# One unrolled phase for the convolution-style attention layer and the token attention with its dispatch

## The reference

```python
x = _L0_conv_ref(x, ...)                    # window attention, 8 heads
x = _L1_conv_ref(x, ...)                    # this change
t = _to_tokens(x)
t = t + _L2_attn_ref(_ln_t(t))              # this change
t = t + _L2_ffn_ref(_ln_t(t), ...)          # routing: this change; experts: later phase
t = t + _L3_attn_ref(_ln_t(t), ...)
t = t + _L3_ffn_ref(_ln_t(t), ...)
...
def _L1_conv_ref(...):
    h_ = group_norm(x, gn_scale, gn_bias)   # 32 groups of 4 channels
    q, k, v = conv1x1(h_, wq, bq), conv1x1(h_, wk, bk), conv1x1(h_, wv, bv)
    attn = softmax(einsum('bci,bcj->bij', q, k) * c ** -0.5)
    return x + conv1x1(einsum('bij,bcj->bci', attn, v), wp, bp)
def _L2_attn_ref(x):
    return softmax(x @ x.T) @ x             # per image, on normalized tokens
def _L2_ffn_ref(...):                       # top 2 of 8 experts, gates by softmax over the two
    topk_vals, topk_idx = top_k(x @ Wg + bg, 2)
```

## Time and profile before

| | |
|---|---|
| median of 3 runs | 2289.88 us (2289.37 to 2290.26) |
| span of the profiled execution, first to last instruction | 2284.1 us |
| PE, DVE, ACT, POOL busy, share of the span | 78%, 71%, 61%, 62% |
| conv phase, from its first ACT instruction to that of d2 | 391.87 to 561.50 us |
| d2 phase, to the first ACT instruction of moe2 | 561.50 to 877.17 us |

### The profile page before, as it was taken

One profiled execution on the slowest core, in us unless ns is written; L12 is line 12 of the kernel. 1 busy time (PEld: TensorE's weight loads), 2 busy tenths in 40 slices (PEclk: granted clock), 3 DMA queues, 4 the chain that ended last, 5 costly groups with the idle time before them and its releaser, 6 DMA issues. The chain is left out here.

```text
span 2284.1 us, 52612 instructions
## 1 busy us (share of the span) xinstructions
PE 1787.9 (78%) x16257; PEld 1236.1 (54%) x16257; DVE 1618.3 (71%) x4634; ACT 1404.3 (61%) x3208; POOL 1414.1 (62%) x1485
## 2 busy tenths in 40 slices
PE   7999997998777744777764777777786299999974
PEld 3555554776566643555543344444444177777763
DVE  5888887787677643666654588888786378888864
ACT  5777775564666523555540788888885267777750
POOL 3655554010177773777776378888888557767765
PEclk9999998999989857999985898998897599999995
DMA  6000000000221134666647012111110367777748
GB/s 116 17 0 0 0 0 2 1 0 18 74 83 55 55 89 124 185 180 179 174 122 249 9 60 68 55 56 55 60 36 30 98 222 232 227 231 234 226 131 338
DMA packets 169828, 233.57 MB, mean 102 GB/s; under 512 B 60032, under 2 KB 131957, under 8 KB 162190
## 3 DMA queue, kind: packets, MB, share of 16 engines
q1 hardware_dynamic: 142446, 172.32, 25.2%
q0 software_dynamic: 26880, 52.27, 6.8%
q10 hardware_dynamic: 288, 6.42, 0.7%
HBM read 155.37 MB, written 79.23 MB: 103 GB/s over the span
## 5 line engine op out<-in xcount | busy, mean ns | idle before, releaser
L2682 POOL DMA_INDIRECT expert_out<-moe_yr,moe_to x448 | 493.0, 1100 | 259.8 <-DVE moe_yr L2661 139.2
L1558 POOL DMA_INDIRECT expert_rows<-d_row,d_pos x392 | 380.8, 971 | 181.9 <-issue 164.8
L2597 ACT ACTIVATE moe_ah<-moe_hps,moe_w 128x512 f32<-128x512 f32 (+1 forms) x336 | 230.2, 685 | 204.3 <-PE moe_hps L2547 199.6
L2638 DVE TENSOR_TENSOR moe_hl<-moe_ah,moe_hh 128x512 fp32r<-128x512 f32 (+1 forms) x336 | 235.2, 700 | 95.6 <-ACT moe_hh L2602 89.3
L1775 PE MATMUL scales_ptps<-ident,scales_pr 113*128 113x113 f32 x512 | 104.2, 306 | 98.1 <-DVE scales_sc L1873 62.5
L550 POOL TENSOR_TENSOR window_pr<-window_pr,window_rc 113x392 f32<-113x392 f32 x128 | 108.9, 851 | 107.3 <-DVE window_rc L494 107.3
L2545 PE MATMUL moe_hps<-moe_xh,moe_w 128*128 128x512 f32 (+1 forms) x336 | 138.3, 412 | 35.5 <-DMA moe_w<-moe_split 31.4
L2533 PE MATMUL moe_xps<-ident,moe_xb 128*128 128x128 f32 x448 | 72.5, 286 | 102.6 <-DMA moe_xb<-expert_rows 102.6
L1775 PEld LDWEIGHTS scales_ptps<-ident,scales_pr 113*128 113x128 f32 x512 | 65.3, 157 | 152.3 <-DVE scales_sc L1873 68.7
L2557 PE MATMUL moe_yps<-moe_hh,moe_w 128*128 128x512 f32 (+1 forms) x336 | 144.3, 429 | 0.9 <-DVE moe_hl L2638 0.9
L538 POOL TENSOR_TENSOR window_sc<-window_sc,window_mx 113x392 f32<-113x392 f32 x128 | 107.8, 842 | 50.6 <-DVE window_mx L468 49.8
(11 more groups left out here) (286 smaller groups left out, 5218.5 us busy)
## 6 DMA issues: line engine op xcount, KB each, us to landing
moe_w<-moe_split SPq DMA_DIRECT2D x56, 1026.5 KB
moe_xb<-expert_rows SPq DMA_DIRECT2D x112, 264.0 KB, 3.0
moe_w<-moe_split SPq DMA_DIRECT2D x56, 449.5 KB
c_yy<-expert_out SPq DMA_DIRECT2D x28, 448.0 KB, 7.1
final_yy<-expert_out SPq DMA_DIRECT2D x28, 448.0 KB, 7.7
expert_out<-moe_yr,moe_to POOLq DMA_INDIRECT x448
X<-in_x SPq DMA_DIRECT2D x32, 196.0 KB
expert_rows<-d_row,d_pos POOLq DMA_INDIRECT x392
```

The costliest lines, as they stand in the source:

```text
L1558: pool.indirect_dma_start(out=self.rows_dram, out_offset=bass.IndirectOffsetOnAxis(ap=self.pos[j][:, i, k:k + 1], axis=0), in_=self.row[j] ...
L2597: act.activation(ah[n % NH][0:P, :], hps[n % 3][0:P, :], func, bias=bias(b, k)[0:P]).then_inc(h_done, 1)
L2638: dve.tensor_tensor(hl[n % NH][0:P, :], ah[n % NH][0:P, :], hh[n % NH][0:P, :].bitcast(F32), ALU.subtract).then_inc(hl_done, 1)
L2682: pool.indirect_dma_start(out=y_dram, out_offset=bass.IndirectOffsetOnAxis(ap=to[j][:, t:t + 1], axis=0), in_=yr[j][:, t, :], in_offset=No ...
```

## The change

Both phases become one, `conv_tokens_phase`, written out step by step: 46 steps (`LAST = NG + 14`), in each of which every engine has one fixed list of items of both layers and of the dispatch. The token attention of a group starts when conv's residual of that group is done. Further edits go with it:

- The chunks have 3 tiles (32 of them, and one of 2), in four rings of row buffers. `turn` makes the rows and the logits in one matmul (`joint`, 136 columns), and the logits' own matmuls are gone.
- The product with the values becomes 8 matmuls per group and layer: four over the even images (rows 0 to 48) and four over the odd ones (rows 64 to 112), 49 columns each, in two items (`values_even`, `values_odd`). `turned` is one copy instead of 4.
- conv's statistics and the values' product share the bank `st`; queries and keys share `pj`, so keys wait for the copy of the queries; the values of both layers share `vps`.
- The token attention subtracts a constant in the exponential instead of the row's maximum; the maximum and the subtraction on DVE are gone there.
- POOL gets conv's normalization, the probabilities of both layers and the low halves of the split weights. conv's copy of the values goes from DVE to ACT.

```diff
-CHUNKS_D2 = chunks_of([4] * 24 + [2])
-CHUNKS_D3 = chunks_of([3] * 32 + [2])
+CHUNKS = chunks_of([3] * 32 + [2])
...
-            single_phase(nc, sh, "conv", conv)
-        token_dispatch_phase(nc, sh, "d2", MOE2, w2, rows_dram)
+            conv_tokens_phase(nc, sh, conv, "d2", MOE2, w2, rows_dram)
...
+        d = Dispatch(nc, sh, sb, sem, kind, e, wsplit, rows_dram, CHUNKS, [sorted_], sorted_[:, 3 * (C + EXPERTS):], joint=True, rings=4)
...
+            def var(g):
+                if not group(g):
+                    return
+                pe.wait_ge(cen_done, min(g + 2, NG))
+                after(pe, res_done, g - 4)
+                pe.wait_ge(ssum_done, g + 1)
+                pe.matmul(st[:, 0:GI], sh.group_w[:, :], ssum[g % 2][:, :], start=True, stop=True).then_inc(var_done, 1)
...
+            def values_odd(g):
+                if not group(g):
+                    return
+                pe.wait_ge(pv_half, g + 1)
+                for b in range(1, GI, 2):
+                    m, q = b // 4, b % 4 // 2
+                    last = pe.matmul(st[:, b * N:(b + 1) * N], vt[g % 4][B1:R, b // 2, :],
+                                     pt[g % 4][B1:R, q * R + B1 * m:q * R + B1 * m + N], start=True, stop=True, skip_group_check=True)
+                last.then_inc(pv_mm, 1)
...
+            for s in range(LAST):
+                var2(s - 9)
+                values_even(s - 8)
+                tokens(s - 7)
+                values_odd(s - 8)
+                turn2(s - 10)
+                var(s - 3)
+                turn(s - 7)
+                queries(s - 4)
+                mean2(s - 8)
+                values2_even(s - 10)
+                scores2(s - 9)
+                values2_odd(s - 10)
+                ranks(s - 11)
+                mean(s - 1)
+                scores(s - 5)
+                keys(s - 4)
+                tokens2(s - 9)
+                turn_rows(s - 10)
+            d.totals(pe)
...
+            for s in range(LAST):
+                if s == 4:
+                    d.prepare(dve)
+                sums(s)
+                if chunk(s - 11):
+                    d.stats(dve, s - 11)
+                residual(s - 8)
+                norm2(s - 9)
+                if chunk(s - 11):
+                    d.scale(dve, s - 11)
+                    d.choose(dve, s - 11)
+                    d.count_up(dve, s - 11)
+                total(s - 6)
...
+            for s in range(LAST):
+                norm(s - 1)
+                scatter(s - 10, 2)
+                probs(s - 4)
+                scatter(s - 9, 0)
+                probs2(s - 7)
+                scatter(s - 9, 1)
+                if group(s - 1) and s - 1 < EXPERTS:
+                    d.split_low(pool, s - 1)
+            d.all_sent(pool)
```

More of the change, by code:

```diff
@@ new lines, in keys, with tokens @@
+            def keys(g):
+                if not group(g):
+                    return
+                pe.wait_ge(q_done, g + 1)
+                pe.matmul(pj[:, 0:T], w[:, C:2 * C], xn[g % 4][:, :, 0:N], start=True, stop=True).then_inc(k_mm, 1)
+            def tokens(g):
+                if not group(g):
+                    return
+                after(pe, v_done, g)
+                after(pe, v2_done, g - 2)
+                for mq in range(4):
+                    two = xn[g % 4][:, 2 * mq:2 * mq + 2, :].rearrange("c b n -> c (b n)")
+                    last = pe.matmul(vps[:, mq, :], two, wvp[:, :], start=True, stop=True, skip_group_check=True)
+                last.then_inc(v_mm, 1)
@@ L2248, in scores @@
+            def scores(g):
+                if not group(g):
+                    return
+                after(pe, sub_done, g)
+                after(pe, t_done, g - 1)
+                pe.wait_ge(k_done, g + 1)
                 for p in range(PAIRS):
@@ new lines, in scores2 @@
+            def scores2(g):
+                if not group(g):
+                    return
+                after(pe, t2_done, g)
+                pe.wait_ge(xn2_done, g + 1)
+                for p in range(PAIRS):
+                    for m, rows in ((0, B1), (1, N)):
+                        b = 4 * m + p
+                        last = pe.matmul(sps2[B1 * m:B1 * m + rows, p * N:(p + 1) * N], xn2[g % 4][:, b, 0:rows], xn2[g % 4][:, b, 0:N],
+                                         start=True, stop=True, skip_group_check=True)
+                last.then_inc(s2_mm, 1)
@@ new lines, in values2_odd @@
+            def values2_odd(g):
+                if not group(g):
+                    return
+                pe.wait_ge(pv2_half, g + 1)
+                for b in range(1, GI, 2):
+                    m, q = b // 4, b % 4 // 2
+                    last = pe.matmul(st2[:, b * N:(b + 1) * N], vt2[g % 4][B1:R, b // 2, :],
+                                     pt2[g % 4][B1:R, q * R + B1 * m:q * R + B1 * m + N], start=True, stop=True, skip_group_check=True)
+                last.then_inc(pv2_mm, 1)
@@ L2406, in turned @@
             def turned(g):
+                if not group(g):
+                    return
+                after(act, pv_mm, g - 3)
                 act.wait_ge(t_mm, g + 1)
[L2408 to L2414 removed]
```

929 lines of the change are left out of this document (375 added, 554 removed).

## The result

The changed kernel takes 2310.26 us (median of 4 runs, 2309.27 to 2318.41) against 2289.82 us (2289.37 to 2290.26) before: a ratio of 1.0105 with a 95% interval of 1.0081 to 1.0129. By the medians it is 0.9% slower; the forecast was 2243 us, and 2195 to 2285 us as its range. The phase itself is 505.4 us long against 485.3, 20.1 us more, about the difference of the medians (20.4).

What follows compares the result with a forecast made beforehand. It took PE to bound conv and POOL's row of scatters d2; 11, 43.5, 300, 39, 29 and 15 us made a phase of 438 against 485.3, so 2284.1 - 47 + 5.8 = 2243 us, range 2195 to 2285.

Steps and rivals of the forecast that it cites:

- 25 x 12.0: Steady steps 11 to 35 of the fused phase: 25 steps of 12.0 us each, 300 us together.
- the granted clock falls: Rival, chance 0.12: many small matmuls and PE standing every step lower the clock; at 30% slow work 2318 us.
- its own sign of being wrong: The prediction called itself wrong if the clock in the steady part was below 0.9.
- The step at full clock: PE's list in a steady step: 11.25 us of work plus 0.64 of wait, taken as 12.0 us.
- Half loads at full price: Values' product on PE: 16 half loads at 0.12 us each, twice before, adding 0.97 us for each layer.
- half price: Rival, chance 0.12: half loads cost half, PE's list is 9.3 us, the step near 10, the kernel 2193 us.
- Change of shape: PE's weights change shape 10 times per step against 4 before: 0.66 us if 0.11 each, else nothing.
- The wait for the residual: PE stands ahead of conv's variance, sharing a bank with the residual, 0.64 us in each step.
- POOL hidden: POOL's list of 9.4 us per step costs nothing as long as PE's longer step covers it.
- The price of a fallen clock: A wholly slow step is about 10 us longer; 1.9 us per step are lost at 19% slow work.
- the rival's even point: A steady step of 13.9 us is where nothing is gained; no change at all had chance 0.04.
- the ends of the phase: Outside the steady steps: 11 and 43.5 us at the start, 39 for steps 36 to 39, then 29 and 15.

Runs made afterwards that it cites:

- e2: The change with conv's variance moved on PE behind the turning and the queries, so PE does not stand for the residual: 2285.02 us, ratio 0.9973.
- e9: The kernel before, phases apart, with only the values' product split into half-row matmuls in conv and d2: 2442.57 us, ratio 1.0709.
- e5: The change with its eight 49-column matmuls per group and layer kept in place, each over 113 rows instead of 49: 2232.63 us, ratio 0.9761.
- e4: The change with the split undone in both layers: four matmuls over 113 rows instead of eight half ones, four copies on ACT: 2181.57 us, ratio 0.9528.
- e11: The change with small and wide items alternating on PE and conv's variance behind the queries: 2310.03 us, ratio 1.0113.
- e12: The change with the token layer's centring matmul issued twice and conv's variance behind the queries: 2290.00 us, ratio 1.0007.
- e10: The change with full rows in both layers, conv's variance behind the token layer's value projection, and conv's root ahead of ACT's copies: 2167.72 us, ratio 0.9457.
- e3: The change with the token layer's centring matmul issued a second time behind the token layer's scores: 2400.33 us, ratio 1.0475.
- e8: The change with full rows in both layers and conv's variance moved behind the queries: 2184.98 us, ratio 0.9535.
- e1: The change with only PE's order altered, so that small and wide items alternate: 2425.55 us, ratio 1.0578.

## Why the prediction was wrong

The step that failed is the clock in the term "25 x 12.0": it priced the steady steps at 1.00, and the rival "the granted clock falls" was put aside at 0.12 by one sentence: conv, "where PE stood under 1% of the time, kept 1.00", and the new step would stand about 5%. The runs showed 0.86 in its place, below the 0.9 that the prediction named as its own sign of being wrong, and 13.84 us per step for 12.14 at full clock: 25 x 1.70 = 42.5 us.

What the rival forecast came true, but not on its condition, that PE stands in every step and holds many small matmuls. e2 and e9 lose the clock with PE standing 0%; e5, with as many small matmuls and a longer stall, keeps 1.00. What e5 takes away is the half rows and, with them, the changes of shape. The rows behind the sentence were of a conv that had no half rows, so they could not speak for a step that has them. That the split is the cause of the loss is shown twice, fused (e4, e5) and phases apart (e9).

Half rows are not the whole condition either: e11 and e12 hold 1.00 and 0.99 with all of them, so order and stall count too. And the kernel before has a phase that speaks against a simple rule by rows or by changes of shape. In window attention PE spends about 141 us on matmuls over 64 rows, between items of other shapes, and keeps 1.00. These have 196 columns, where the halves have 49; whether that is the difference no run shows. Two groups of PE between 25 and 380 us, and the busy time of that stretch (columns as in the earlier trace rows):

```profile
L323 PE MATMUL window_sps<-window_kbd,window_qt 64*64 64x196 f32 x510 | 71.2, 352 | 1.2 <-DVE window_sc L466 1.2
L323 PE MATMUL window_sps<-window_kbd,window_qt 64*49 64x196 f32 x510 | 69.6, 346 | 0.0
```

```profile
25.00:380.00 355.00, 335.30 (x4782) 188.54 (x4786) 301.69 (x630) 261.03 (x528) 211.18 (x251) 1.00 0.07 14
```

Point by point:

- **The step at full clock** (12.0 us): right in the number, 12.14 us measured, its last 0.7 us already at the lower level; but by luck, since errors cancel. The list without the added changes of shape is 10.79 us (e5) where 11.25 was forecast, these changes add 0.93 where nothing was, and the wait is 0.42 instead of 0.64. With full rows e4 has 9.70 less 0.57 of stall, 9.1, where the forecast list of 11.25 less 1.94 for the split gives 9.3.
- **Half loads at full price** (0.97 us for 8): right in kind, 0.83 between full-size items in e5; the 1.02 of the change hold the changes of shape as well. The rival "half price" is dead: 187 ns for 49 rows, 192 for 113.
- **Change of shape**: left at nothing in the 12.0 us, 0.66 at most. The change and e5 differ by 0.93 us per step (11.72 - 10.79), which I put down to it, so of these two values 0.66 was the nearer.
- **The wait for the residual**: right in place and kind. PE stands 0.42 us (0.64 forecast), and the residual begins 0.04 us behind the odd half's last matmul, lasts 0.63, and the variance follows 0.1 us later. That this wait has a second price, through the clock, was not seen: e2 gains 25 us by its removal, and the 25 waits themselves are 10.5 of them.
- **POOL hidden**: right; 99.48 of 180 us busy. In e10 the step is 9.28 us, near the 9.4 us forecast for POOL's list. Scatters began 69.8 us after the phase's start (65 forecast).
- **The price of a fallen clock**: the rival's even point, 13.9 us, was right too. At 13.84 us the steady part alone would have left about no change; it is 346.1 - 300 = 46.1 us over the forecast, 42.5 of them by the clock. The rest comes from the ends of the phase: 5.0 us at the start, 10.7 in steps 36 to 39 and 6.1 behind them, where the clock is low as well (0.67 between 820 and 860 us). With full rows (e4) the ends take 54.7, 33.0 and 47.9 us, 135.6 for the 137.5 forecast, so the split accounts for most of this rest too, though how much of it is clock the runs do not part. 46.1 + 5.0 + 10.7 + 6.1 = 67.9 us, the whole miss of 505.4 - 437.5.

What stays open: whether the rows or the changes of shape let the clock fall, and why one fall lasts 3.4 us, another 13.7 in the same kernel, and 17 us in e3. The runs show at which items falls begin, that without half rows there are none in the steady part of the fused phase (1.00 from 460 to 640 us in e4, e5, e8 and e10), and that without the stall the long ones are rare there (one of 13.65 us in e11, none in e2 and e12); no run shows what ends one.

## What to carry to other kernels

Price an edit on TensorE at both levels of its clock (1.00 and 0.50 here), and do not split a matmul by rows without a reason: half the rows saved nothing in time (a load of 49 rows took 187 ns, one of 113 rows 192), and here the split cost 129 us against three copies per layer on an engine that had room. Of the 4.15 us between the steady steps of the change and of e4, 1.66 are the added loads (10.79 - 9.13), 0.93 the changes of shape, 1.70 the clock, and -0.15 the shorter stall. When a change bundles a gain and a loss, undo the parts one by one: the fusion with its other edits was worth 108 us and stood hidden behind the split. A removed wait is judged by the step's new length, not by its own: in e8 PE's wait for the residual went, POOL's wait for the root stayed, and the step kept its 9.7 us.

## What the runs showed of the hardware that was not expected

The granted clock fell to its lower level, 0.50, again and again in conv with PE busy 140.00 of 140 us, where matmuls over 49 rows stood (e9: 0.50 from 463 to 465 us, 0.85 on average), and in the fused phase with PE busy 180.00 of 180 us (e2: 0.50 from 491 to 494 us, 0.91 on average). In the fused phase it stayed at 1.00 with the same number of matmuls and columns over 113 rows (e5; 0.86 in the change). So in these runs a gap in which PE stands was not needed for a fall, though a short one (0.42 us) went with a lower clock (0.65 in e1 with the gap, 1.00 in e11 without). Adding a wide matmul to each step, 0.85 us from its start to the next item's (550.41 - 549.56 in e3), moved the clock from 0.86 to 0.71, and with the stall gone to 0.99: the place of one matmul of 8 columns was worth 110 us there.
